# Causal masks of the attention scores: matmuls on TensorE replaced by GpSimd's selects for units 0 to 2, and two products with the values one part later

## Chip, core and metric

The kernel runs on one core of a Trainium2 chip. The metric is the device time of one execution in microseconds (us). Five engines work at once, each with its own queue in program order: TensorE (PE, its weight loads PEld), VectorE (DVE), ScalarE (ACT), GpSimd (POOL) and SyncE (SP, which issues the DMAs). They wait for each other through semaphores.

## The reference

A layer over x of shape (16, 1024, 256), fp32: a state-space block, a gated feed-forward block, attention, and the feed-forward block again, each on the layer-normed x and added to it. The change lies in the attention:

```python
x_proj = x @ Wqkv + bqkv
q = x_proj[:, :, :C].reshape(B, n_head, T, hd)          # C 256, n_head 16, hd 16, T 1024
k = x_proj[:, :, C:2 * C].reshape(B, n_head, T, hd)
v = x_proj[:, :, 2 * C:].reshape(B, n_head, T, hd)
att = jnp.einsum('bhtd,bhsd->bhts', q, k) * (1.0 / jnp.sqrt(jnp.float32(hd)))
causal = jnp.tril(jnp.ones((T, T), dtype=bool))
att = jnp.where(causal, att, jnp.float32(-jnp.inf))
att = jax.nn.softmax(att, axis=-1)
y = att @ v
y = jnp.transpose(y, (0, 2, 1, 3)).reshape(B, T, C)
return y @ Wproj + bproj
```

Since the reshape has no transpose before it, a "head" is a stretch of 64 tokens with 16 pieces of each token as its rows, 1024 rows of 16 numbers in all.

## The kernel before

`attention_phase` works in 64 **slots**, four (q = 0 to 3) for each of 16 **batches** b; a slot handles four heads, in two row groups g of TensorE with two heads p each. Two passes over the causal scores run at once. Pass 1 (`first_piece`, L1981) makes the scores of a later slot with queries on the partitions, and VectorE takes their row maxima (`maxima`, L1737 and L1740); the maxima are turned and moved by DMA into a row of the query stack. Pass 2 (`second_piece`, L2001) makes this slot's scores with keys on the partitions, less the row maximum; ScalarE takes the exponentials (`exponentiate`, L1862) into the tiles `probs`, of which there are three sets (PROBS = 3), used by units in turn. TensorE multiplies these with the values (`times_v`, L2029) into one PSUM bank, `o_ps`.

Pass 2 of a slot has nine **units** (PASS2): stretches of a key block against queries, 512 columns together. Each is done four times (p and g), so a slot has 36 score pieces and 36 exponentials, in 18 steps of two. Units 0, 1, 2, 7 and 8 touch the diagonal, where keys lie above the query within a block of 128. There, before the change, two more small bf16 matmuls per piece (`masked`, L1951) add -1e30 in PSUM above the diagonal: 40 in a slot. Units 0 and 7 have one such block, units 1, 2 and 8 two (128 moving columns in place of 64). Exponentials then become 0.

TensorE's order is written out by hand in its `slot`: behind every third pair of score pieces a **part** ends (12 parts, 0 to 11). There stands at most one **step** of other work through the single bank `x_ps` (`x_events`: transposes of the heads, of y, the output product, the eight projection steps j = 0 to 7 of a later half batch), and then, where TIMES_V_SLOTS says so, a unit's product with the values. Before, units 0 to 7 stand at the parts 2, 3, 4, 5, 7, 8, 10, 11, unit 8 at part 0 of the next slot. The second piece of unit 2 is multiplied with unit 3. ScalarE or VectorE empties `x_ps` after each step and frees it for the next. A unit's exponentials may overwrite `probs` only when the product of three units before is done; for unit 5 that is unit 3's product, since it reads the rest of unit 2.

Projection steps 0 and 1 transpose the normed x, ScalarE copies that to `full`, and GpSimd rounds it to a high part (L1550) and subtracts (L1552, `split`); step 2 (`project`, L2056) waits on TensorE for both splits. GpSimd's queue is another hand-written order, sorted by a place counted in steps: splits, the values' bias (L1616), the residual's bias (`bias`, L1621, behind a DMA), layer norm of x (L1535) and the lay-outs (L1564) that turn the staged q and k for a slot further on, each after its own DMA. ScalarE, VectorE and SyncE are sorted in the same way.

## Time and profile before

| | us |
|---|---|
| median of 3 runs | 3762.44 (3750.83 to 3772.56) |
| the profiled execution | 3763.16 |
| its span, first to last instruction | 3761.3 |
| TensorE busy, of the span | 3560.0 (95%) |
| VectorE busy | 2952.9 (79%) |
| ScalarE busy | 2183.7 (58%) |
| GpSimd busy | 1666.4 (44%) |

The attention stage lies between some 1060 and 3140 us of the span. A batch of four slots takes about 128 us in its steady middle. "Busy" of TensorE is modelled from starts, and overlapping matmuls count once; so the distance from one instruction's start to another's is the better measure of what TensorE does. Idle time of an engine stands before the instruction that ended it, with what released it.

### The profile page before, as it was taken

What the parts mean: (1) busy time and instruction counts of PE and PEld (TensorE: products, weight loads), DVE (VectorE), ACT (ScalarE), POOL (GpSimd) and SP (SyncE); (2) the same over time, 40 slices, a digit from 0 to 9 for tenths busy, and PEclk for the clock granted to TensorE, in tenths of its full rate; (3) what the DMA queues carried; (4) which work ended last, traced back from release to release, by engine and by line L of the source; (5) the groups of instructions that cost most, each with busy time, mean ns of one, the idle gap of its engine ahead of it and who ended that gap; (6) DMA issues with size and microseconds to landing.
All of it is one profiled execution on the core that took longest, in us unless ns stands there. A gap on an engine that the chain in (4) does not pass through costs nothing. (4 is left out here: it accounts for less than half of the span.)

```text
span 3761.3 us, 76026 instructions
## 1 busy us (share of the span) xinstructions
PE 3560.0 (95%) x25550; PEld 2347.9 (62%) x25550; DVE 2952.9 (79%) x9275; ACT 2183.7 (58%) x4151; POOL 1666.4 (44%) x2027
## 2 busy tenths in 40 slices
PE   6999899999689999999999999999999998999997
PEld 5888666666455665566656656655666555666664
DVE  8998666766688888888888888888888893676775
ACT  1110456655337766766676667667667665656654
POOL 2332123223345556656555565565565511223323
PEclk9999899999879999999999999999999999999999
DMA  2333112111497978787887879788887832121211
GB/s 74 100 98 109 57 46 68 54 59 35 116 140 111 126 115 129 120 127 123 122 127 119 132 116 126 116 119 123 124 134 121 120 41 80 40 68 46 68 46 45
DMA packets 694291, 361.16 MB, mean 96 GB/s; under 512 B 297905, under 2 KB 660913, under 8 KB 693937
## 3 DMA queue, kind: packets, MB, share of 16 engines
q1 hardware_dynamic: 693936, 356.62, 53.5%
q8 instruction: 200, 3.28, 0.4%
q14 instruction: 155, 1.26, 0.2%
HBM read 204.49 MB, written 150.99 MB: 95 GB/s over the span
## 5 line engine op out<-in xcount | busy, mean ns | idle before, releaser
L1862 ACT ACTIVATE att_probs<-att_s 128x512 f32<-128x512 f32 x2304 | 1212.5, 601 | 461.2 <-PE att_s L2001 234.4
L1737 DVE CUSTOM_DVE_ANT_0 att_s<-att_s,att_above 128x384 f32<-128x384 f32 (+3 forms) x2048 | 950.2, 519 | 132.8 <-PE att_s L1981 127.1
L1981 PE MATMUL att_s<-att_ks,att_qs 48*128 48x512 f32 (+3 forms) x3072 | 896.0, 401 | 5.7 <-DVE att_maxima L1740 3.6
L2001 PE MATMUL att_s<-att_qs,att_ks 49*128 49x512 f32 (+3 forms) x3072 | 852.4, 373 | 20.5 <-DVE att_maxima L1737 5.2
L2001 PEld LDWEIGHTS att_s<-att_qs,att_ks 49*128 49x128 f32 x3072 | 487.6, 186 | 464.0 <-ACT att_probs L1862 271.6
L1740 DVE TENSOR_REDUCE att_maxima<-att_s 128x1 f32<-128x512 f32 x1024 | 661.9, 684 | 98.3 <-PE att_s L1981 93.2
L2029 PE MATMUL att_o_ps<-att_probs,att_vs 128*32 128x512 f32 (+3 forms) x6144 | 620.5, 497 | 25.1 <-ACT att_probs L1862 22.1
L1981 PEld LDWEIGHTS att_s<-att_ks,att_qs 48*128 48x128 f32 x3072 | 485.9, 189 | 26.4 <-DVE att_maxima L1737 8.9
L1097 PE MATMUL ffn_h2p<-ffn_h,ffn_w 128*128 128x512 f32 x768 | 365.0, 598 | 3.0 <-ACT ffn_h L968 0.9
L1951 PE MATMUL att_s<-att_mask,att_places 64*128 64x128 bf16 (+1 forms) x2560 | 327.7, 212 | 0.0
L1737 DVE DVE_READ_ACCUMULATOR2_ANT att_maxima<- 128x1 f32 x2048 | 293.0, 143 | 0.0
L946 ACT ACTIVATE ffn_uv<-ffn_uvp 128x512 f32<-128x512 f32 x256 | 153.1, 598 | 237.5 <-PE ffn_uvp L1072 237.5
L2029 PEld LDWEIGHTS att_o_ps<-att_probs,att_vs 128*32 128x32 f32 x6144 | 145.9, 108 | 222.9 <-issue 159.6
L1564 POOL CAST att_qs<-att_staged 113x1024 fp32r<-113x1024 f32 x128 | 253.7, 2005 | 0.0
L976 ACT ACTIVATE ffn_h<-ffn_turned,ffn_b 128x512 f32<-128x512 f32 x384 | 241.9, 684 | 13.5 <-PE ffn_turned L1088 11.6
L1564 POOL CAST att_ks<-att_staged 113x1024 fp32r<-113x1024 f32 x126 | 249.7, 2000 | 0.0
L968 ACT ACTIVATE ffn_h<-ffn_h2p,ffn_b 128x512 f32<-128x512 f32 x192 | 132.0, 687 | 197.8 <-PE ffn_h2p L1097 197.8
L1088 PEld LDWEIGHTS ffn_turned<-identf,ffn_uv 128*128 128x128 f32 x1536 | 174.8, 142 | 75.5 <-issue 53.9
L158 ACT ACTIVATE ssm_xnT<-ssm_turned 128x512 fp32r<-128x512 f32 x64 | 34.9, 595 | 313.7 <-PE ssm_turned L166 313.7
L1088 PE MATMUL ffn_turned<-identf,ffn_uv 128*128 128x128 f32 x1536 | 201.8, 274 | 10.2 <-DVE ffn_uv L823 8.0
L823 DVE SCALAR_TENSOR_TENSOR ffn_uv<-ffn_uv,ffn_c_pos 128x256 f32<-128x256 f32 x512 | 209.3, 483 | 2.3
L691 POOL TENSOR_TENSOR ffn_var_eps<-ffn_moments,ffn_eps 128x4 f32<-128x4 f32 x64 | 13.3, 208 | 433.4 <-DVE ffn_moments L776 433.4
(292 smaller groups left out, 6384.8 us busy)
## 6 DMA issues: line engine op xcount, KB each, us to landing
att_staged<-qk_scratch SPq DMA_DIRECT2D x768, 128.0 KB, 7.6
qk_scratch<-att_parts SPq DMA_DIRECT2D x128, 512.0 KB, 3.4
ffn_x<-x SPq DMA_DIRECT2D x64, 512.0 KB, 5.2
ssm_x<-in_L_attn_a_x_dram SPq DMA_DIRECT2D x32, 512.0 KB, 3.7
x<-ssm_y SPq DMA_DIRECT2D x32, 512.0 KB, 3.0
x<-ffn_y SPq DMA_DIRECT2D x32, 512.0 KB, 2.9
att_x<-x SPq DMA_DIRECT2D x32, 512.0 KB, 7.4
v_scratch<-att_v_tok SPq DMA_DIRECT2D x32, 512.0 KB, 5.3
```

Source lines behind the costliest of these rows:

```text
L823: last = v.scalar_tensor_tensor(out=new[:, t, 0:D], in0=old[:, t, D:2 * D], scalar=c_pos[i][j][:, t, k:k + 1], in1=old[:, t, 0:D], op0=ALU ...
L976: last = a(h1[k][:, f, :], turned_ps[:, f, :], ACT.Gelu, bias=b1[:, f:f + 1])
L1088: last = pe.transpose(turned_ps[:, f, t * P:(t + 1) * P], of[:, t, f * P:(f + 1) * P], identf[:, :])
L1097: last = mm(h2_ps[:, :], w2[:, f, :], h1[k][:, f, :], start=(f == 0), stop=(f == KT - 1))
L1564: last = g.tensor_copy(stack[0:ROWS, :].rearrange("p (t c) -> p t c", c=HD)[:, e * n:(e + 1) * n, :], staged[side][0:ROWS, :, e * n:(e + 1 ...
L1737: last = v.tensor_tensor_reduce(scores, scores, above[:, CH - w:CH], 1.0, -3.0e38, ALU.add, ALU.max, to)
L1740: last = v.tensor_reduce(to, scores, AX.X, ALU.max)
L1862: a(probs[u % PROBS][2 * g + p][:, 0:n], bank[:, 0:n], ACT.Exp).then_inc(exp_done, 1)
L1951: last = mm(blocks[:, at, GROUP * half:GROUP * (half + 1)], places[rows, 2 * (1 - k) + half, :], mask[rows, 1 - k, 0:len(cols), :], start= ...
L1981: last = mm(bank[:, col:col + w], rows_of(qs[buf], g, KROWS, p, BT * blk, BT * (blk + 1)), rows_of(ks[buf], g, KROWS, p, t0, t1), start=k ...
L2001: last = mm(bank[:, col:col + w], rows_of(ks[buf], g, SHIFT + 1, p, BT * j, BT * (j + 1)), rows_of(qs[buf], g, SHIFT + 1, p, t0, t1), star ...
L2029: last = mm(o_ps[32 * i:32 * i + 32, HD * (t0 - first_t):HD * (t1 - first_t)], vs[s][:, NBLK * head + j, :], probs[of % PROBS][i][:, col:c ...
```

## The change

For units 0, 1 and 2 of every slot (SELECTED) the two mask matmuls of a piece are gone, and `stop` moves to the last score matmul. In their place GpSimd sets the entries above the diagonal of the exponentials in `probs` to zero, one `affine_select` in place for each of the 12 pieces (`keep_causal`), behind a wait for the exponential, at a place 1.4 steps behind it in GpSimd's order. `times_v` of these units waits for the selects and no longer for the exponentials. Units 7 and 8 keep their mask matmuls.

The products of units 3 and 5 move from parts 5 and 8 to parts 6 and 9. The steps through `x_ps` that stood at parts 6 and 9 move to parts 5 and 8 (one from 8 to 7), and with them their copies, splits, additions and stores on the other queues. The residual's bias in the second slot of a batch moves from place 4 to 7.1 on GpSimd, and the first two lay-outs from 6.3 and 7.6 to 7.2 and 8.2.

```diff
+    SELECTED = ((0, 1, 2),) * 4
-    PROBS = 3
+    PROBS, KEPT_BEHIND = 3, 1.4
-    TIMES_V_SLOTS = {2: 0, 3: 1, 4: 2, 5: 3, 7: 4, 8: 5, 10: 6, 11: 7}
+    TIMES_V_SLOTS = {2: 0, 3: 1, 4: 2, 6: 3, 7: 4, 9: 5, 10: 6, 11: 7}
-    LAY_OUT_AT, LAY_OUT_BEHIND_X_AT, PIECES = (6.3, 7.6, 10.2, 12.2), (8.2, 8.4, 11.2, 11.4), 2
+    LAY_OUT_AT, LAY_OUT_BEHIND_X_AT, PIECES = (7.2, 8.2, 10.2, 12.2), (8.2, 8.4, 11.2, 11.4), 2
-        finish = [] if first else {0: [(3, "turn", 0), (6, "out", 0), (7, "turn", 1), (9, "out", 1), (10, "turn", 2)],
-                                   1: [(1, "out", 2), (2, "turn", 3), (6, "out", 3)]}.get(q, [])
-        project = {0: [(1, 6), (4, 7)], 1: [(4, 0), (7, 1), (9, 2)], 2: [(1, 3), (4, 4), (6, 5), (9, 6)],
+        finish = [] if first else {0: [(3, "turn", 0), (5, "out", 0), (7, "turn", 1), (8, "out", 1), (10, "turn", 2)],
+                                   1: [(1, "out", 2), (2, "turn", 3), (5, "out", 3)]}.get(q, [])
+        project = {0: [(1, 6), (4, 7)], 1: [(4, 0), (7, 1), (8, 2)], 2: [(1, 3), (4, 4), (5, 5), (8, 6)],
                    3: [(1, 7)]}[q] if more else []
-        project += [(2, 0), (4, 1), (6, 2), (8, 3), (9, 4), (11, 5)] if q == 3 and more2 else []
+        project += [(2, 0), (4, 1), (5, 2), (7, 3), (8, 4), (11, 5)] if q == 3 and more2 else []
...
+                def keep_causal(quad, step, g):
+
+                    u, p = step // 2, step % 2
+                    pool.wait_ge(exp_done, 2 * STEPS * quad + 2 * step + g + 1)
+                    cols = diagonals(PASS2[u], False)
+                    m = blocks_at(probs[u % PROBS][2 * g + p][:, :], cols)
+                    nc.gpsimd.affine_select(out=m, in_=m, pattern=[[0, len(cols)], [1, P]], compare_op=ALU.is_ge, fill=0.0,
+                                            base=0, channel_multiplier=-1).then_inc(causal_kept, 1)
...
-                        tasks += [((17.5, 4)[q], lambda: bias(b - 1, 2 + q))]
+                        tasks += [((17.5, 7.1)[q], lambda: bias(b - 1, 2 + q))]
...
+                    for of, units, ahead in ((quad - 1, SELECTED[(q - 1) % 4], STEPS), (quad, SELECTED[q], 0)):
+                        for step, group in itertools.product((2 * u + p for u in units for p in range(2)), range(2)):
+                            at = step + group / 2 + KEPT_BEHIND - ahead
+                            if of >= 0 and (at >= 0 if ahead else at < STEPS):
+                                tasks += [(at, lambda of=of, step=step, group=group: keep_causal(of, step, group))]
...
-                              stop=k == len(PASS2[u]) - 1 and not diagonals(PASS2[u], False))
+                              stop=k == len(PASS2[u]) - 1 and (u in SELECTED[buf] or not diagonals(PASS2[u], False)))
                     if k == len(PASS2[u]) - 1:
-                        if diagonals(PASS2[u], False):
+                        if diagonals(PASS2[u], False) and u not in SELECTED[buf]:
                             last = masked(bank[:, :], 1, g, diagonals(PASS2[u], False))
...
-                    pe.wait_ge(exp_done, 2 * STEPS * quad + 4 * u + 4)
+                    if u in SELECTED[q]:
+                        pe.wait_ge(causal_kept, kept_before(quad, u) + 4)
+                    else:
+                        pe.wait_ge(exp_done, 2 * STEPS * quad + 4 * u + 4)
```

## Rows read from the trace of the kernel before

**Rows 1.** The page: busy time of the engines, and two costly groups.
```profile
PE 3560.0 (95%) x25550; PEld 2347.9 (62%) x25550; DVE 2952.9 (79%) x9275; ACT 2183.7 (58%) x4151; POOL 1666.4 (44%) x2027
...
L1862 ACT ACTIVATE att_probs<-att_s 128x512 f32<-128x512 f32 x2304 | 1212.5, 601 | 461.2 <-PE att_s L2001 234.4
...
L1564 POOL CAST att_qs<-att_staged 113x1024 fp32r<-113x1024 f32 x128 | 253.7, 2005 | 0.0
```

**Rows 2.** Sums over one steady batch; columns: stretch, length, engines' busy us, clock, DMA.
```profile
1860.23:1988.60 128.37, 125.57 (x1116) 77.65 (x1112) 111.58 (x374) 89.88 (x171) 76.87 (x68) 1.00 0.83 124
```

**Rows 3.** Timeline of TensorE, second slot, parts 3 to 6: start, length, engine, what, count.
```profile
1901.67 0.38 PE L2001 MATMUL att_s<-att_qs,att_ks 49*128 49x256 f32 x1
...
1902.88 0.66 PE L2070 MATMUL att_x_ps<-identf,att_o 128*128 128x128 f32 x4
...
1904.47 0.50 PE L2001 MATMUL att_s<-att_qs,att_ks 49*128 49x512 f32 x1
...
1905.43 0.55 PE L2052 MATMUL att_x_ps<-identf,att_x 128*128 128x128 f32 x3
...
1907.23 0.50 PE L2001 MATMUL att_s<-att_qs,att_ks 49*128 49x512 f32 x1
...
1908.60 1.50 PE L2029 MATMUL att_o_ps<-att_probs,att_vs 128*32 128x512 f32 x16 [0.40 <-ACT att_probs L1862]
...
1910.03 0.50 PE L2001 MATMUL att_s<-att_qs,att_ks 49*128 49x512 f32 x1
```

**Rows 4.** The same timeline, parts 8 and 9.
```profile
1916.35 1.07 PE L2029 MATMUL att_o_ps<-att_probs,att_vs 128*32 128x512 f32 x8
...
1917.35 0.50 PE L2001 MATMUL att_s<-att_qs,att_ks 49*128 49x512 f32 x1
...
1918.77 0.50 PE L2056 MATMUL att_x_ps<-att_xnT,att_wqkv 128*128 128x512 f32 x1
```

**Rows 5.** The mask products, grouped by line: duration ns min/median/max.
```profile
L1951 PE MATMUL att_s<-att_mask,att_places x2560: 190/216/327, 1082.8 to 3134.2; 64*128 64x128 bf16 x119, 64*128 64x64 bf16 x78
```

**Rows 6.** Sums as in rows 2, over parts 0 to 3 of the first and third slot.
```profile
1860.23:1871.34 11.11, 11.11 (x126) 7.80 (x122) 10.18 (x31) 7.84 (x15) 3.03 (x3) 1.00 0.90 125
...
1924.87:1935.37 10.50, 10.50 (x118) 6.96 (x114) 9.69 (x33) 7.34 (x14) 2.91 (x4) 1.00 1.22 140
```

**Rows 7.** Selects and copies of GpSimd by group, then GpSimd's and VectorE's timeline.
```profile
L53 POOL TENSOR_SCALAR_AFFINE_SELECT identf<-identf 128x128 f32<-128x128 f32 x1 | 0.3, 296 | 0.2 <-POOL identb L50 0.2
...
L1535 POOL TENSOR_SCALAR att_x<-att_x,att_moments,att_rstd 128x256 f32<-128x256 f32 x116 | 140.9, 1222 | 3.1
...
1036.62 2.40 DVE L1712 CAST att_ks<-att_staged 113x2048 fp32r<-113x2048 f32 x1
...
1036.92 2.27 POOL L1601 TENSOR_SCALAR_AFFINE_SELECT att_mask<-att_mask 64x128 bf16<-64x128 bf16 x1
```

**Rows 8.** Timelines of TensorE and GpSimd, fourth slot, parts 4 and 5.
```profile
1968.23 0.66 PE L2052 MATMUL att_x_ps<-identf,att_x 128*128 128x128 f32 x4
...
1969.38 0.49 PE L2001 MATMUL att_s<-att_qs,att_ks 49*128 49x512 f32 x1
...
1971.00 1.28 PE L2029 MATMUL att_o_ps<-att_probs,att_vs 128*32 128x512 f32 x12 [0.32 <-ACT att_probs L1862]
...
1965.16 1.28 POOL L1552 TENSOR_TENSOR att_xnT<-att_full,att_xnT 128x512 fp32r<-128x512 f32 x1
...
1970.63 1.27 POOL L1552 TENSOR_TENSOR att_xnT<-att_full,att_xnT 128x512 fp32r<-128x512 f32 x1
```

**Rows 9.** Timelines of TensorE and GpSimd, second slot: transposes of step 1 and its split.
```profile
1913.87 0.66 PE L2052 MATMUL att_x_ps<-identf,att_x 128*128 128x128 f32 x4
...
1916.26 1.28 POOL L1552 TENSOR_TENSOR att_xnT<-att_full,att_xnT 128x512 fp32r<-128x512 f32 x1
```

**Rows 10.** Timelines of GpSimd and TensorE, third slot, part 3.
```profile
1931.90 1.28 POOL L1552 TENSOR_TENSOR att_parts<-att_full,att_parts 128x512 fp32r<-128x512 f32 x1
...
1934.36 1.07 PE L2029 MATMUL att_o_ps<-att_probs,att_vs 128*32 128x384 f32 x16
```

More of the change, by code:

```diff
@@ L4 @@
 from contextlib import ExitStack
+import itertools
 import numpy as np
@@ L1331, in attention_phase @@
          xn_ready, x_full, x_free, hi_ready, parts_ready, v_ready, v_stored, s1_full, s1_free, row_max_ready,
-         row_max_turned, s2_full, exp_done, pv_done, o_free, recip_ready, bias_added, tail_full, y_done, yT_done, out_added) = [sem("att_" + n) for n in (
+         row_max_turned, s2_full, exp_done, pv_done, o_free, recip_ready, bias_added, tail_full, y_done, yT_done, out_added, causal_kept) = [sem("att_" + n) for n in (
              "low_free v_free wq_loaded loaded const_ready zero_max weights_ready mask_zero mask_ready above_ready rounded split_done stats_done moments_done eps_added rstd_ready "
              "xn_ready x_full x_free hi_ready parts_ready v_ready v_stored s1_full s1_free row_max_ready "
-             "row_max_turned s2_full exp_done pv_done o_free recip_ready bias_added tail_full y_done yT_done out_added").split()]
+             "row_max_turned s2_full exp_done pv_done o_free recip_ready bias_added tail_full y_done yT_done out_added causal_kept").split()]
         wq_raw = y_sb[:, :, :, :].rearrange("p f n d -> p (f n d)")[:, 0:KT * 3 * D].rearrange("p (k n) -> p k n", k=KT)
@@ L1372, in s2_use, with kept_before, diagonals, blocks_at @@
             return 2 * STEPS * q + 2 * step + g
+        def kept_before(quad, u):
+            of = [4 * len(units) for units in SELECTED]
+            units = SELECTED[quad % 4]
+            return sum(of) * (quad // 4) + sum(of[:quad % 4]) + (4 * units.index(u) if u in units else 0)
+        def diagonals(unit, end):
+            cols, col = [], 0
+            for blk, t0, t1 in unit:
+                w = HD * (t1 - t0)
+                if (t1 == BT * (blk + 1)) if end else (t0 == BT * blk):
+                    cols.append(col + w - P if end else col)
+                col += w
+            return cols
+        def blocks_at(bank, cols):
+            at = slice(cols[0] // P, cols[-1] // P + 1, max(1, (cols[-1] - cols[0]) // P))
+            return bank.rearrange("p (n w) -> p n w", w=P)[:, at, :]
         def in_order(tasks):
@@ L1668, in _ @@
                 run(pool, sequence)
+                for step, group in itertools.product((2 * u + p for u in SELECTED[3] for p in range(2)), range(2)):
+                    if step + group / 2 + KEPT_BEHIND >= STEPS:
+                        keep_causal(4 * NB - 1, step, group)
                 for r in range(4):
@@ L1953, in masked @@
                     return last
-                def diagonals(unit, end):
-                    cols, col = [], 0
-                    for blk, t0, t1 in unit:
-                        w = HD * (t1 - t0)
-                        if (t1 == BT * (blk + 1)) if end else (t0 == BT * blk):
-                            cols.append(col + w - P if end else col)
-                        col += w
-                    return cols
                 def first_wait(quad, unit, g):
```

## The prediction

> **What bounds the kernel now.** I read the page first [rows 1], then the sums of one steady batch [rows 2], then TensorE's own timeline, part by part [rows 3]. The page says TensorE 95%. The batch sums say it for the stage that the change touches: of 128.37 us TensorE is busy 125.57, VectorE 111.58 (87%), ScalarE 89.88, GpSimd 76.87 (60%), clock 1.00 throughout. So the time of a batch is TensorE's list of work plus its waits, and VectorE stands right behind it. Sixteen such batches (64 slots) are the attention stage. Nothing before or behind it changes.
>
> In the timeline I take the distance from the first score product of a part to the first instruction behind the scores. Part 3 of the second slot goes from 1901.67 to 1902.88: 1.21 us with six mask products. Part 4 has none: 1904.47 to 1905.43, 0.96. Part 5 has none either and takes 1907.23 to 1908.60, 1.37: 0.41 us of wait for exponentials, in front of unit 3's product with the values, which then runs 1.43 us, until 1910.03 [rows 3]. Part 9 has four masks of 64 columns and takes 1.42 us, from 1917.35 to 1918.77 [rows 4], where 0.96 and some 0.1 for the masks would do: 0.36 of wait. The part before it held only scores and one product with the values (1916.35 to 1917.35 [rows 4]), 1.9 us in all, while VectorE's share of a batch is 111.58 / 48 = 2.3 us a part. There are five waits of this kind in a batch, at parts 8 and 9, of 0.35 to 0.48. These two kinds of wait are what the moves of the products and steps touch.
>
> **The change, part by part** (us for the four slots of a batch; minus is a gain).
>
> *Masks removed.* 24 of 40 mask products per slot, all in parts 0 to 3. A mask is listed with 0.19 us or more [rows 5], but they overlap, so I price the part: 1.21 - 0.96 = 0.25 for six masks of 128 columns [rows 3]. Parts 0 and 1 hold narrower ones; I price them by columns at 0.16 and 0.22. Sum 0.88 a slot, 3.5 a batch, if TensorE sets the pace there. VectorE speaks against all of it: in parts 0 to 3 it is busy 9.69 of 10.50 us in the third slot and 10.18 of 11.11 in the first (the second is the same kind, the fourth looser) [rows 6]. Less 0.88 the third slot would have 9.62 us for 9.69 of work. So I take back 0.4 in the third slot, 0.3 in the second, 0.1 in each other one: **-2.6**, bounds -3.5 (all) and -1.5 (VectorE needs its usual gaps too).
>
> The Trainium skill ("TensorE: Matmul & The Clock Gate", Back-to-back issue gap) gives N/2.4 + 2.5 ns for one product behind another, 29 and 56 ns at 64 and 128 columns: by it 8 and 16 masks would be worth 1.1 us a slot. The rows say 0.25 for six, some 42 ns each, less than its 56; by the page the term would be -4.5 before VectorE's part.
>
> *Unit 3's product one part later.* Its 0.41 of wait goes in three slots; in the fourth it is larger: scores from 1969.38, product at 1971.00, 1.62 against 0.96 [rows 8]. **-1.9**. Cover: the exponentials it needs are then a whole part old.
>
> *A new wait behind it.* The exponential of unit 5's first piece must not overwrite the probabilities that unit 3's product still reads (second piece of unit 2, same buffer). That exponential is the last of part 6, and the product is now at the end of part 6: it starts 0.96 + 1.43 + 0.1 = 2.5 us into the part instead of after 1.6. It takes 0.6 [rows 1], done at 3.1; the third score piece of part 7 wants its bank two thirds into that part's scores, at about 2.4 + 0.6 = 3.0. Bounds 0 and 0.4 a slot, I take 0.2 (the bank waits for the semaphore too): **+0.8**.
>
> *Short parts.* Part 8 now holds an output, a projection step or the like, part 9 is short instead. The five waits at parts 8 and 9 come to 2.0; behind the new part 9 (1.07 + 1.0, a little longer than 1.9) and the third slot's short parts 6 and 7 I expect 1.0 in all to be left: **-1.0**, bounds 0 and -1.6.
>
> *Steps one part earlier.* In the second slot the projection step 2 moves from part 9 to 8, in the fourth from 6 to 5. Each needs GpSimd's split of step 1, which sits in the part just before. Fourth slot: step 1's transposes start at 1968.23, ScalarE's copy and GpSimd's cast and subtraction end at 1970.63 + 1.27 = 1971.90, 3.67 us later; TensorE's scores of part 5 would be over at 1969.38 + 0.96 = 1970.34 [rows 8]. It waits 1.6. Second slot: from the transposes at 1913.87 to the end of the subtraction at 1916.26 + 1.28 is 3.67 too [rows 9], 1917.54; the scores of part 8 were over at 1916.35 [rows 4], so 1.2, and 0.7 more, my estimate, since GpSimd's bias and four lay-outs of 2.0 us [rows 1] now begin behind the selects. **+3.5**, bounds +2.8 and +4.3. The other moved steps only need the shared PSUM bank, freed well within a part: 0; uncovered, a copy's 0.6 us each.
>
> *Selects on GpSimd.* 12 a slot. A select of 128x128 fp32 took 296 ns; for the eight with two blocks I take 0.49, an estimate between once and twice that, bounds 0.3 and 1.22 (another operation on 128x256) [rows 7]. That is 5.2 us a slot, 76.87 + 20.8 = 98 of 128: it fits. Who waits is TensorE's unit product. Unit 0 to 2's products come a part behind their last exponential, 2 us or more. Only where GpSimd is held is it close: third slot, split until 1931.90 + 1.28 = 1933.18, then three selects to 1934.65, product at 1934.36 less the masks' gain [rows 10]: 0.3 and more, part of it in place of a wait that the next part has now; I take 0.3. Fourth slot: split until 1965.16 + 1.28 = 1966.44, four selects to 1968.4, product half a microsecond before the scores of 1969.38, less the gain [rows 8]: 0.1. **+0.4**, bounds 0 and +6.
>
> *Bias and lay-outs behind the selects.* The lay-outs are needed a slot later, the bias only by the output in part 5; before, GpSimd sat idle for that load. 0. Semaphores and their queue: nothing else stands behind the waiting product but the next scores, priced above.
>
> **Sum.** -2.6 - 1.9 + 0.8 - 1.0 + 3.5 + 0.4 = -0.8 a batch. Fifteen batches: -12. The last has no projection: its slots save 4 us. The profiled execution took 3763.16 us (span 3761.3), within 1 us of the median 3762.44; minus 16 that is 3747, and 3746 against the median.
>
> **Rivals.**
> *A. TensorE keeps the whole gain.* VectorE has slack in the other parts and three banks to run ahead, so the masks bring 3.5, the short parts 1.0, unit 3 1.9, and the exponential's new wait is hidden; the splits still cost 3.5: -2.9 a batch, 15 x 2.9 + 4 = 48, **3714**. For it: VectorE at 87%. Against: VectorE's 9.69 of 10.50.
> *B. VectorE becomes the bound and the splits add (slower).* Place: parts 0 to 3, where VectorE is 91 to 92% busy, and the splits at parts 5 and 8. Masks -1.5, unit 3 -1.9, short parts 0, exponential +0.8, splits +4.3, selects +0.8: +2.5 a batch, **3797**. It decides once splits and selects cost more than the 4.5 that masks, unit 3 and short parts bring; the step 1 to step 2 gap in the fourth slot shows it.
> *C. GpSimd is late.* If the two-block select takes 1.22 us, four behind the split in the fourth slot end at 1971.3, 2.5 behind the product, as in the third slot, and 1 in the second: +6 a batch, **3835**. It starts at 0.6 a select. For it: one 64x128 select took 2.27 us, beside siblings of 0.3. But it began at 1036.92 inside VectorE's copy from SBUF to SBUF (1036.62, 2.40 long) and ended with it [rows 7], and in the steady batches VectorE reads mostly PSUM.
> The Trainium skill ("SBUF — State Buffer", Who interferes with whom) has it as a rule: VectorE in a two-port mode shuts GpSimd out for a whole instruction, with at most one SBUF input and no such mode it does not. By it C would need such copies; the trace's 2.27 agrees.
> *D. Nothing to see,* as waits only move: 3762.
>
> **How the numbers follow.** Forecast (about 3730 to 3760) 0.42; A 0.27; B 0.21; C 0.06; D 0.04. Faster than 3743.6 (0.5%, about what a measurement here can tell) is A and a third of the forecast's case: 0.42. Within 0.5%: the rest of the forecast, D, and a little of B: 0.36. Slower: 0.22. The range goes from just under A to just under B's price, 3706 to 3792; the likeliest case's own range is 3728 to 3762.
>
> **What would show it.** Right: parts 0 to 3 without masks near 1.0 us; no wait before unit 3's product; TensorE idle 1 to 2 us before the projection step 2, ended by GpSimd's subtraction; selects of 0.3 and 0.5 us; VectorE over 88% of the batch. Wrong: step 2 starting without a wait, selects over 0.6 us, products of units 0 to 2 waiting for selects in every slot, or the slots shorter by a whole microsecond each.

## The result, and the profile after

The changed kernel takes 3775.99 us (median of 20 runs, 3764.94 to 3787.72), the kernel before 3764.92 beside it (20 runs): ratio 1.0028, with 95% between 1.0019 and 1.0037. So it is 0.3% slower, a difference that is certain in its sign and smaller than the 0.5% of the prediction's bound. The forecast was 3746 us, a small gain. The profiled execution took 3777.97 us with a span of 3775.6; the one before, 3763.16 with 3761.3.

The page of the kernel after, busy times with the clock line, and the group of the selects:

```profile
PE 3549.2 (94%) x24014; PEld 2289.0 (61%) x24014; DVE 2958.7 (78%) x9275; ACT 2182.9 (58%) x4151; POOL 1926.7 (51%) x2795
...
PEclk9999899999779999999989999999999988999999
...
L1641 POOL TENSOR_SCALAR_AFFINE_SELECT att_probs<-att_probs 128x256 f32<-128x256 f32 (+1 forms) x768 | 272.6, 369 | 358.2 <-ACT att_probs L1903 345.2
```

TensorE has 1536 instructions fewer than in [rows 1], 24 in each of 64 slots, yet is busy only 10.8 us less, and the span is 14 us longer. VectorE and ScalarE do what they did. GpSimd is busy 260 us more, the selects' 272.6 less some 12 that its other work took less. Whether TensorE waits for them is asked in e2 and e8.

The sums over slots, in the form of [rows 2]: the first, third and fourth slot of the batch shown there, and the second of a later batch, which is nearer to the median:

```profile
1860.56:1892.02 31.46, 31.41 (x272) 19.36 (x268) 28.67 (x96) 22.43 (x43) 21.36 (x27) 1.00 1.04 128
2158.82:2192.53 33.71, 31.66 (x254) 18.47 (x250) 27.95 (x93) 21.84 (x43) 21.51 (x27) 0.95 0.68 110
1931.89:1962.81 30.92, 30.52 (x250) 17.59 (x247) 27.47 (x96) 22.26 (x42) 23.80 (x30) 0.97 0.79 127
1962.81:1997.89 35.08, 33.64 (x266) 19.92 (x262) 27.26 (x92) 23.86 (x45) 26.69 (x34) 0.95 0.52 103
```

The second and the fourth slot are long, and the granted clock there is 0.95, where [rows 2] had 1.00 over the whole batch. (The third has 0.97 here, because the second slot of its batch, one of 39.9 us, ended at half clock.) From the starts of the slots on TensorE's timeline I take the median length of each over batches 1 to 14 and the mean of the whole batch, for the kernels of this study (us; "half" counts stretches in which the granted clock was 0.50):

| kernel | slot 1 | 2 | 3 | 4 | sum of medians | mean batch | half |
|---|---|---|---|---|---|---|---|
| before | 32.75 | 31.47 | 30.89 | 33.47 | 128.58 | 129.38 | 3 |
| after | 31.46 | 33.75 | 30.01 | 35.07 | 130.29 | 129.93 | 19 |
| e1, step 2 back | 31.46 | 33.05 | 30.01 | 35.23 | 129.75 | 129.43 | 21 |
| e2, masks only | 31.98 | 30.77 | 30.82 | 32.74 | 126.31 | 126.09 | 0 |
| e3, moves only | 32.24 | 32.15 | 30.08 | 34.30 | 128.77 | 129.33 | 5 |
| e4, wait filled | 31.46 | 32.34 | 30.01 | 33.55 | 127.36 | 127.14 | 1 |
| e5, mixed | 31.47 | 30.76 | 30.00 | 32.74 | 124.97 | 124.77 | 0 |
| e6, split later | 31.98 | 30.76 | 30.82 | 32.74 | 126.30 | 126.14 | 1 |
| e7, tail masks | 31.99 | 30.75 | 30.82 | 32.74 | 126.30 | 126.09 | 0 |
| e8, selects twice | 32.09 | 31.66 | 34.09 | 36.86 | 134.70 | 134.43 | 26 |
| e9, measured later | 31.39 | 30.77 | 30.41 | 32.75 | 125.32 | 125.07 | 1 |
| e10, both later | 31.41 | 30.77 | 30.04 | 32.74 | 124.96 | 124.65 | 0 |

The means add up to the span: 14 x (129.93 - 129.38) = 7.7 us, and the last batch, 119.4 against 113.3, gives 6.1; 13.8 of the 14.3 us between the two spans. The medians tell what the usual slot does. The two differ because the execution of before has a few long batches (131.9 and 133.9 against 128.6), and because not every slot of after is long. That the clock is lower is no accident of the one profiled execution: over the whole span it is 0.962 to 0.969 in all 20 executions of the changed kernel, and 0.974 to 0.980 in the 23 executions of the kernel before that stood beside e1 to e4.

Slots 1 and 3 gained 1.3 and 0.9; slots 2 and 4, where the projection step 2 moved forward, lost 2.3 and 1.6. The timelines of TensorE and GpSimd over parts 5 and 6 of a fourth slot show how (the places of [rows 8]):

```profile
1974.16 0.66 PE L2086 MATMUL att_x_ps<-identf,att_x 128*128 128x128 f32 x4
...
1975.41 0.49 PE L2032 MATMUL att_s<-att_qs,att_ks 49*128 49x512 f32 x1
...
1977.98 2.90 PE L2090 MATMUL att_x_ps<-att_xnT,att_wqkv 128*128 128x512 f32 x6 [1.36 <-POOL att_xnT L1576]
1980.81 0.73 PE L2032 MATMUL att_s<-att_qs,att_ks 49*128 49x512 f32 x1
...
1973.30 1.49 POOL L1641 TENSOR_SCALAR_AFFINE_SELECT att_probs<-att_probs 128x256 f32<-128x256 f32 x4
1975.87 0.61 POOL L1574 CAST att_xnT<-att_full 128x512 fp32r<-128x512 f32 x1 [1.09 <-ACT att_full L1913]
1976.57 1.26 POOL L1576 TENSOR_TENSOR att_xnT<-att_full,att_xnT 128x512 fp32r<-128x512 f32 x1
```

From the transposes of step 1 (1974.16) to the end of GpSimd's subtraction (1976.57 + 1.26 = 1977.83) it is 3.67 us, the prediction's number, and TensorE starts step 2 right behind it, after 1.36 us of idle time. That is the forecast wait. What was not forecast is the length of step 2 itself: 2.83 us until the next scores at 1980.81. Sums over the two stretches:

```profile
1975.40:1977.90 2.50, 1.22 (x12) 0.85 (x8) 2.49 (x10) 2.37 (x5) 1.94 (x3) 1.00 0.33 106
1977.98:1980.81 2.83, 2.83 (x7) 1.80 (x8) 0.22 (x2) 0.00 (x0) 2.83 (x2) 0.50 0.00 0
```

During the wait the granted clock is still 1.00. Behind it, while TensorE is busy without a gap, it is 0.50, which is 1.2 GHz in place of 2.4. The waits in this trace between 1110 and 2900 us (total, times, longest):

```profile
PE att_x_ps L2090 <- POOL att_xnT L1576: 48.2, 28, 2.8
```

28 waits, 1.7 us on average, two a batch: 1.36 us in every fourth slot, 1.97 to 2.76 in every second one. Before, no such wait is in the list. In batches 1 to 14 there are 27 of them, and behind 18 the clock falls: 10 of 13 in fourth slots, 8 of 14 in second ones. A fourth slot in which it stays up is 33.6 us long in place of 35.1, and step 2 in it takes 1.56 us.

### The profile page after: what moved, and what is told of

Read it like the earlier page. It is cut to its first block and busy times, and to the rows that moved or that the text cites. A ratio compares the mean times of both kernels' runs of the same rounds, so it can differ in the third digit from the quotient of the medians.

```text
span 3775.6 us, 73723 instructions
## 1 busy us (share of the span) xinstructions
PE 3549.2 (94%) x24014; PEld 2289.0 (61%) x24014; DVE 2958.7 (78%) x9275; ACT 2182.9 (58%) x4151; POOL 1926.7 (51%) x2795
## 5 line engine op out<-in xcount | busy, mean ns | idle before, releaser
L2012 PE MATMUL att_s<-att_ks,att_qs 48*128 48x512 f32 (+3 forms) x3072 | 880.4, 397 | 6.7 <-DVE att_maxima L1781 4.3
L2032 PEld LDWEIGHTS att_s<-att_qs,att_ks 49*128 49x128 f32 x3072 | 471.6, 190 | 508.9 <-ACT att_probs L1903 317.9
L2063 PE MATMUL att_o_ps<-att_probs,att_vs 128*32 128x512 f32 (+3 forms) x6144 | 628.5, 504 | 6.7 <-POOL att_probs L1641 6.0
L2012 PEld LDWEIGHTS att_s<-att_ks,att_qs 48*128 48x128 f32 x3072 | 475.9, 192 | 26.1 <-DVE att_maxima L1778 9.0
L1641 POOL TENSOR_SCALAR_AFFINE_SELECT att_probs<-att_probs 128x256 f32<-128x256 f32 (+1 forms) x768 | 272.6, 369 | 358.2 <-ACT att_probs L1903 345.2
L2090 PE MATMUL att_x_ps<-att_xnT,att_wqkv 128*128 128x512 f32 x714 | 216.2, 442 | 50.1 <-POOL att_xnT L1576 50.1
L970 ACT ACTIVATE ffn_h<-ffn_h2p,ffn_b 128x512 f32<-128x512 f32 x192 | 131.9, 687 | 198.5 <-PE ffn_h2p L1099 198.5
```

The costliest lines, as they stand in the source:

```text
L1641: nc.gpsimd.affine_select(out=m, in_=m, pattern=[[0, len(cols)], [1, P]], compare_op=ALU.is_ge, fill=0.0, base=0, channel_multiplier=-1).t ...
L2012: last = mm(bank[:, col:col + w], rows_of(qs[buf], g, KROWS, p, BT * blk, BT * (blk + 1)), rows_of(ks[buf], g, KROWS, p, t0, t1), start=k ...
L2032: last = mm(bank[:, col:col + w], rows_of(ks[buf], g, SHIFT + 1, p, BT * j, BT * (j + 1)), rows_of(qs[buf], g, SHIFT + 1, p, t0, t1), star ...
L2063: last = mm(o_ps[32 * i:32 * i + 32, HD * (t0 - first_t):HD * (t1 - first_t)], vs[s][:, NBLK * head + j, :], probs[of % PROBS][i][:, col:c ...
L2090: last = mm(bank[:, :], wq[i][:, f, cols], xnT[k][:, f, :], start=(n == 0), stop=(n == KT * len(PARTS_R) - 1))
```

## The experiments

The theory: the moves brought step 2 so close to its split that TensorE stands still, and the stop costs twice, as a wait and as half a clock behind it. Rivals: the selects delay the products (C of the prediction); the new exponential wait or the busy VectorE is what costs (B). The runs of e1 to e4 stood beside a median of 3754.97 us for the kernel before, e5 to e8 beside 3762.07, e9 and e10 beside 3764.04, so compare by ratio across these groups.

**e1: the changed kernel with step 2 back at its old parts.**

```diff
-        project = {... 1: [(4, 0), (7, 1), (8, 2)], ...
-        project += [(2, 0), (4, 1), (5, 2), (7, 3), (8, 4), (11, 5)] if q == 3 and more2 else []
+        project = {... 1: [(4, 0), (7, 1), (9, 2)], ...
+        project += [(2, 0), (4, 1), (6, 2), (7, 3), (8, 4), (11, 5)] if q == 3 and more2 else []
```

> The changed kernel, with only projection step 2 put back one part later (part 9 in the second slot, part 6 in the fourth). Theory S (the loss is TensorE's wait for GpSimd's split of step 1, and the half clock that follows it): both waits go, TensorE's clock stays at 1.00 in the steady batches, second slot about 31 us and fourth about 33; a batch goes from 130.3 to some 125 us, the kernel to about 3710 us, 1.5% below before. Rival G (GpSimd's selects hold up products or VectorE): the waits in front of step 2 go, but the slots stay near 33 and 34 us, and the kernel stays at 3765 to 3776 us.

Measured: 3751.32 us, ratio 0.9986 (0.9973 to 0.9999), where some 3710 was expected of the theory. The wait for the split is gone but for three second slots, the half clock is not (21 stretches), and slots 2 and 4 stay long at 33.05 and 35.23. The profiled execution is the slowest of its 12 (3769.68 us), but the clock over the span is 0.961 to 0.971 in all of them. The timeline of TensorE and two sums in e1's fourth slot, part 5, which now holds scores only, and part 6:

```profile
1963.31 0.50 PE L2032 MATMUL att_s<-att_qs,att_ks 49*128 49x512 f32 x1 [0.23 <-ACT att_probs L1903]
...
1964.07 0.46 PE L2032 MATMUL att_s<-att_qs,att_ks 49*128 49x512 f32 x1 [0.26 <-DVE att_maxima L1778]
...
1964.83 0.76 PE L2032 MATMUL att_s<-att_qs,att_ks 49*128 49x512 f32 x1 [0.26 <-ACT att_probs L1903]
...
1965.67 2.93 PE L2090 MATMUL att_x_ps<-att_xnT,att_wqkv 128*128 128x512 f32 x6
1968.52 2.79 PE L2063 MATMUL att_o_ps<-att_probs,att_vs 128*32 128x512 f32 x16
```
```profile
1964.00:1967.50 3.50, 3.16 (x9) 2.23 (x10) 2.65 (x10) 1.22 (x3) 3.50 (x4) 0.58 0.00 0
1967.50:1972.00 4.50, 4.50 (x24) 1.41 (x22) 0.10 (x1) 0.56 (x2) 0.74 (x1) 0.56 0.00 0
```

So my edit took one wait away and made others: with neither a product nor a step in part 5, TensorE runs into the exponentials and the row maxima, three waits of a quarter of a microsecond within 1.6 us, and the clock is at half around and behind these too. Step 2 takes 2.85 us again and unit 3's product, 1.43 in [rows 3], takes 2.7. It does not isolate the wait for the split, then; what it shows is that the clock also falls where TensorE waits for something else.

**e2: the masks alone** (selects, their waits and the places of bias and lay-outs, with the old order of products and steps). **e3: the moves alone** (the kernel before with the new order).

```diff
# e2, from the changed kernel; e3 puts the lines marked - into the kernel before
-    TIMES_V_SLOTS = {2: 0, 3: 1, 4: 2, 6: 3, 7: 4, 9: 5, 10: 6, 11: 7}
+    TIMES_V_SLOTS = {2: 0, 3: 1, 4: 2, 5: 3, 7: 4, 8: 5, 10: 6, 11: 7}
-        finish, project = ...    # the lists of x_events, new
+        finish, project = ...    # the lists of x_events, as before
```

> Only the selects in place of the masks (with the places of GpSimd's bias and lay-outs that belong to them); products with the values and all steps through x_ps stand as before the change. Theory S: the selects are free and the masks' time comes off, 0.5 to 0.7 us a slot; about 3725 to 3735 us. Rival G: products wait for selects and GpSimd's splits come late; 3760 us or more. If VectorE is the bound of parts 0 to 3, less than 0.3 us a slot: 3750 us.

> The kernel before with only the products of units 3 and 5 one part later and the steps through x_ps one part earlier; masks on TensorE as before, no selects. Theory S: the second and fourth slot wait 1.2 to 1.7 us in front of projection step 2, the clock halves for a few us behind it, slots one and three gain 0.4 to 0.6; about 3810 us, slower than the changed kernel. Rival G: without selects the moves gain what was meant, 3740 us or less, and there is no half clock.

Measured: e2 3714.00 us, ratio 0.9885 (0.9869 to 0.9900); e3 3767.21, ratio 1.0030 (1.0020 to 1.0041). The two halves have opposite signs. The masks alone bring 1.15%: per slot 0.77, 0.70, 0.07 and 0.73 us, 2.27 a batch. (1.15% is 43 us, 2.9 a batch: before also has stops and three stretches at half clock in its steady batches, and e2 has none of the latter, so the mean batches differ by 3.3.) The moves alone bring 0.5 in slot 1 and 0.8 in slot 3 and lose 0.7 and 0.8 in slots 2 and 4; their loss is far from the 3810 that was expected. Their waits, over the same stretch:

```profile
PE att_x_ps L2056 <- POOL att_xnT L1552: 36.5, 28, 2.0
```

28 waits again, but the clock falls behind only 4 of the 27 in batches 1 to 14. In second slots the wait is mostly 1.1 us, not 2.0, and none of these 14 waits is followed by half clock. What is shorter there is GpSimd's side: from the transposes of step 1 to the end of the subtraction it is 3.5 us, against 4.4 in the changed kernel, while TensorE's scores of part 8 begin 1.58 us behind those transposes in both. GpSimd's timeline, a second slot of the changed kernel, then one of e3, which keeps bias and lay-outs at their old places:

```profile
2177.03 3.95 POOL L1588 CAST att_ks<-att_staged 113x1024 fp32r<-113x1024 f32 x2
2180.94 0.60 POOL L1574 CAST att_xnT<-att_full 128x512 fp32r<-128x512 f32 x1
```
```profile
1781.63 1.99 POOL L1564 CAST att_ks<-att_staged 113x1024 fp32r<-113x1024 f32 x1
1784.39 0.61 POOL L1550 CAST att_xnT<-att_full 128x512 fp32r<-128x512 f32 x1 [0.77 <-ACT att_full L1872]
```

ScalarE's copy of step 1 ends at 2179.98 in the first and at 1784.33 in the second. With the lay-outs behind the selects, the split of step 1 stands behind one of them for 0.96 us; in e3 it starts at once. These 0.9 us are the prediction's 0.7 for the second slot.

In fourth slots the wait is the same 1.36 us, and 4 of 13 are followed by half clock, against 10 with the masks gone. This is a count in one execution each, but the clocks of all executions agree: over the span 0.971 to 0.976 in the 12 of e3, 0.962 to 0.969 in the 20 of the changed kernel. So the length of the wait is not all that decides. The two halves of the change work against each other: 126.31 + 128.77 - 128.58 would be 126.5 a batch, and together they take 130.3. Slot by slot the same sum gives 31.5, 31.5, 30.0 and 33.6; the changed kernel has 31.5, 33.8, 30.0 and 35.1, so all of the difference lies in the two slots with the waits.

**e4: the changed kernel, with twelve transposes of the identity in front of step 2's wait.** They go into `x_ps`, and step 2 overwrites them.

```diff
+                            for n in range(12):
+                                pe.transpose(bank[:, (n % 4) * P:(n % 4 + 1) * P], identf[:, :], identf[:, :])
                             (before the wait for the split in step 2)
```

> The changed kernel with 12 transposes of the identity into the idle x_ps bank (some 1.7 us of work) in front of the wait for the split before each projection step 2 in the slots; nothing else moves, what they write is overwritten. Theory S with the clock as a part of its own: the wait stays as long (the engine is now busy in it), the half-clock stretches of 3.4 us behind it mostly vanish, step 2 takes 1.6 us and not 2.8; about 25 us less than the changed kernel, 3750. Rival (the clock is no cause, only the wait counts): the same time as the changed kernel or, by what the transposes outlast the split, up to 20 us more.

Measured: 3733.13 us, ratio 0.9938 (0.9921 to 0.9954), 0.9% or some 34 us under the changed kernel by the ratios, although TensorE has 348 instructions more. The clock over the span is 0.973 to 0.978 in its six executions. TensorE's timeline, parts 5 and 6 of a fourth slot:

```profile
1953.26 0.50 PE L2032 MATMUL att_s<-att_qs,att_ks 49*128 49x512 f32 x1
...
1954.38 1.53 PE L2084 MATMUL att_x_ps<-identf 128*128 128x128 f32 x12
1955.73 1.65 PE L2092 MATMUL att_x_ps<-att_xnT,att_wqkv 128*128 128x512 f32 x6
1957.32 0.50 PE L2032 MATMUL att_s<-att_qs,att_ks 49*128 49x512 f32 x1
```

and in front of step 2 in a second slot:

```profile
1900.07 1.53 PE L2084 MATMUL att_x_ps<-identf 128*128 128x128 f32 x12
1902.09 1.67 PE L2092 MATMUL att_x_ps<-att_xnT,att_wqkv 128*128 128x512 f32 x6 [0.49 <-POOL att_xnT L1576]
```

The transposes take 1.35 us, about what the wait took, so step 2 starts no sooner. But it takes 1.59 us in place of 2.83, and there is one stretch at half clock in batches 1 to 14. In the second slot half a microsecond of idle time remains, and the clock stays up too. This separates the two costs: after minus e4, 130.29 - 127.36 = 2.9 us a batch (1.4 in slot 2, 1.5 in slot 4, nothing in the others), is the clock; e4 minus e2, 1.05 a batch, is the moves with their waits. And e4's slots are the sums of the two halves, 31.5, 31.5, 30.0 and 33.6, but for 0.9 more in the second, which is the split behind the lay-out.

**e5: the mixed order.** Selects in all slots, the new order in slots 1 and 3, the old one in 2 and 4.

```diff
-    TIMES_V_SLOTS = {2: 0, 3: 1, 4: 2, 6: 3, 7: 4, 9: 5, 10: 6, 11: 7}
+    TIMES_V_SLOTS = ({2: 0, 3: 1, 4: 2, 6: 3, 7: 4, 9: 5, 10: 6, 11: 7}, {2: 0, 3: 1, 4: 2, 5: 3, 7: 4, 8: 5, 10: 6, 11: 7}) * 2
-                                   1: [(1, "out", 2), (2, "turn", 3), (5, "out", 3)]}.get(q, [])
+                                   1: [(1, "out", 2), (2, "turn", 3), (6, "out", 3)]}.get(q, [])
-        project = {... 1: [(4, 0), (7, 1), (8, 2)], ...
+        project = {... 1: [(4, 0), (7, 1), (9, 2)], ...
-        project += [(2, 0), (4, 1), (5, 2), (7, 3), (8, 4), (11, 5)] if q == 3 and more2 else []
+        project += [(2, 0), (4, 1), (6, 2), (8, 3), (9, 4), (11, 5)] if q == 3 and more2 else []
```

> The changed kernel's order in the first and third slot of a batch only; the second and fourth slot keep the products of units 3 and 5, the output and projection step 2 where they were before the change (masks are selects in all four). Theory W (a slot loses where a part has to wait for the split or is left without other work, and the moves are good where this is not so): slots 31.5, 30.8, 30.0 and 32.7 us, clock 1.00 in the steady batches, a batch 125.0, some 1.3 less than with the masks' change alone; about 3694 us. Rival (the moves' gain in slots one and three is paid back in the slot behind them): 3714 us, as the masks' change alone.

Measured: 3701.58 us (3698.93 to 3702.14), ratio 0.9833 (0.9813 to 0.9853). It beats both kernels, by 60 us the one before; by the ratios some 20 us of that are the order (against e2), the rest are the masks. Sums over the four slots and the batch:

```profile
1833.23:1864.71 31.48, 31.43 (x272) 19.38 (x268) 28.68 (x96) 22.43 (x43) 21.40 (x27) 1.00 1.02 129
1864.71:1895.45 30.74, 30.25 (x254) 17.68 (x250) 27.68 (x93) 21.85 (x43) 21.55 (x27) 1.00 0.64 103
1895.45:1925.84 30.39, 30.00 (x252) 17.09 (x248) 27.98 (x100) 22.26 (x42) 23.83 (x30) 1.00 1.12 163
1925.84:1958.58 32.74, 32.25 (x264) 19.12 (x261) 27.11 (x92) 23.77 (x45) 26.75 (x34) 1.00 0.64 116
1833.23:1958.58 125.35, 123.93 (x1028) 73.26 (x1025) 111.45 (x374) 90.31 (x172) 93.52 (x117) 1.00 0.85 128
```

Each slot has the better of its two lengths and the clock is 1.00 throughout. In the third slot VectorE is busy 27.98 of 30.39 us, the highest share (92%) of the four.

**e6: why the masks bring nothing in the third slot.** e2, with the split of the projection step 3 in the third slot 1.6 steps later on GpSimd, so that it comes behind unit 1's selects. **e9 and e10:** e5 with VectorE's measurements of the next x (`MEASURE_AT`) later, and e9 with the later split too.

```diff
# e6 and e10
-     tasks += [(at + 2, lambda j=which, n=n: split(projected(b, q, j)[0], j, x_base(b, q) + n))]
+     tasks += [(at + (3.6 if (q, which) == (2, 3) else 2), lambda j=which, n=n: split(...))]
# e9 and e10
-    MEASURE_AT, MOMENTS_AT = (2.6, 4.1, 5.6, 7.1), 8.6
+    MEASURE_AT, MOMENTS_AT = (6.1, 7.6, 9.1, 10.6), 11.6
```

> The masks' change alone, with GpSimd's split of projection step 3 in the third slot behind the selects of unit 1 and not before them. If the third slot got only 0.1 us from the masks because unit 1's product waits there for selects that stand behind this split, part 3 of that slot goes from 1.44 to 0.9 us and the slot from 30.8 to 30.3; 15 x 0.5 = 8 us, about 3706 us. Rival (VectorE is the bound of these parts, as the prediction had it): the wait moves to part 4 and the slot stays at 30.8; 3714 us.

> The mixed order (selects in all slots, the moves in the first and third slot only) with VectorE's four statistics instructions of the next x, 0.41 us each, in the first and third slot 3.5 steps later in its queue (places 6.1 to 10.6, moments at 11.6, in place of 2.6 to 7.1 and 8.6). If VectorE is what keeps the third slot from gaining by the masks (its waits of 0.5 in part 3 and 0.2 in part 4), these fall and the slot goes from 30.0 to about 29.5 us, the first slot, without such a wait, stays at 31.5; about 3693 us against 3701 for the mixed order. Rival (selects behind the split are the cause): the slot stays at 30.0, or the wait comes back in parts 7 to 9; 3701 us or more.

> As the run before, and GpSimd's split of projection step 3 in the third slot behind the selects of unit 1. If both VectorE's lag and the selects behind the split hold the third slot, and each alone hides the other, only this one shows the gain: part 3 at 0.95 and part 4 at 1.0 us, the slot at 29.3; about 3690 us. If one of them is the cause alone, it is the same as the run before or as the mixed order.

Measured: e6 3715.72 us, ratio 0.9877 (0.9851 to 0.9902), as e2. TensorE's timeline, third slot, parts 3 and 4, of e2 and then of e6:

```profile
2161.09 0.38 PE L2032 MATMUL att_s<-att_qs,att_ks 49*128 49x256 f32 x1
...
2162.53 1.07 PE L2063 MATMUL att_o_ps<-att_probs,att_vs 128*32 128x384 f32 x16 [0.44 <-POOL att_probs L1641]
2163.53 0.50 PE L2032 MATMUL att_s<-att_qs,att_ks 49*128 49x512 f32 x1
...
2164.72 1.21 PE L2090 MATMUL att_x_ps<-att_xnT,att_wqkv 128*128 128x512 f32 x4
```
```profile
2159.07 0.38 PE L2032 MATMUL att_s<-att_qs,att_ks 49*128 49x256 f32 x1
...
2160.00 1.07 PE L2063 MATMUL att_o_ps<-att_probs,att_vs 128*32 128x384 f32 x16
2161.13 0.47 PE L2032 MATMUL att_s<-att_qs,att_ks 49*128 49x512 f32 x1
...
2162.70 1.66 PE L2090 MATMUL att_x_ps<-att_xnT,att_wqkv 128*128 128x512 f32 x6
```

In e2 unit 1's product waits 0.44 us for the selects; from the scores of part 3 to step 4 it is 3.63 us. In e6 that wait is gone, part 3's scores take 0.93 in place of 1.44, but part 4's take 1.57 in place of 1.19, and from scores to step 4 it is 3.63 again. GpSimd's lateness, forecast at 0.3 us here, is real and costs nothing, since the time comes back as waits in the next part. e9, 3712.92 (0.9866, 0.9842 to 0.9889), has third slots of 30.41, longer than e5's: part 3 waits as in e2, and the relief in part 4 (0.95) comes back in parts 6 and 8 (1.27 and 1.36). e10, 3702.33 (0.9845, 0.9822 to 0.9869), has both edits and 30.04, e5's length to 0.04. So e6 and e10 move the waits and leave the slot as long as it was, and e9 makes it longer. With the moves the slot takes 30.0 us and VectorE is busy 28.0 of it in the median (93%). That VectorE sets the pace there is what these runs speak for; none took work off VectorE, so it is not shown. And it is not the whole answer for the masks alone: in e2 VectorE has the same 27.9 us of work in a slot of 30.8.

**e7: the last batch keeps its masks on TensorE** (e2 otherwise). The last batch of e2 has half clock in 37.5 us of its 124.3, of before in none of 113.3, and the theory was that the lost masks had thinned TensorE's work too far there.

```diff
+        def selected(quad):
+            return SELECTED[quad % 4] if quad < 4 * (NB - 1) else ()
```

> The masks' change alone, but the last batch keeps its masks on TensorE, as before the change. That batch has little other work for TensorE: with selects it took 124.3 us, at half clock for 48 of them, against 113.3 before. If the masks' absence leaves TensorE idle there and the clock follows, the last batch comes back to about 113 us with under 5 us at half clock; about 3704 us. Rival (the half clock there comes from something else, the state of the engine's earlier work): last batch still 120 us or more, 3714 us.

Measured: 3722.25 us, ratio 0.9883 (0.9858 to 0.9908), no better than e2; its last batch took 121.3 us, 20.5 of them at half clock. And e6, which has e2's order in the last batch, took 112.5 us there with 3.4 at half clock. The theory falls: the last batch's clock differs between executions of the same order, each of them profiled once. What decides it stays open; it is a matter of some 12 us that no reading of the steady batches contains.

**e8: each select done twice** (e2 otherwise), the second behind a semaphore of the first.

```diff
-                    nc.gpsimd.affine_select(...).then_inc(causal_kept, 1)
+                    for done in (causal_half, causal_kept):
+                        nc.gpsimd.affine_select(...).then_inc(done, 1)
+                        if done is causal_half:
+                            pool.wait_ge(causal_half, kept_before(quad, u) + 2 * p + g + 1)
```

> The masks' change alone, with each select done twice, the second behind the first's semaphore: about 0.55 us more for each of 12 a slot, 6.6 us a slot, GpSimd at some 95% of a batch. It asks how much cover the selects have. If GpSimd's work is covered up to its time in total, products of units 1 and 2 wait some tenths in the third and fourth slot: 3720 to 3735 us. If what counts is the order in GpSimd's queue (rival C of the prediction), products and splits wait 1 to 2 us in several slots and the clock halves behind them: 3790 us or more.

Measured: 3850.65 us, ratio 1.0225 (1.0200 to 1.0250), by the ratios some 128 us over e2. TensorE's waits for selects, 1110 to 2900 us, in e2 and in e8:

```profile
PE att_o_ps L2063 <- POOL att_probs L1641: 5.7, 13, 0.4
```
```profile
PE att_o_ps L2066 <- POOL att_probs L1642: 58.3, 33, 2.7
```

Single selects leave 5.7 us of waiting between 1110 and 2900 us; a second one makes it 58.3, and there are 26 stretches at half clock, 24 of them close behind such a wait. It falls where the prediction looked for it: slots 3 and 4, by 3.3 and 4.1 us. So rival C is a live mechanism with its point between once and twice the measured select, and the change stays on the good side of it.

## Why the prediction was wrong, point by point

The total missed by 30 us, and the direction with it. Per batch, forecast against measured (differences of the sums of medians, and in brackets of the mean batches, in which before carries its own long ones):

| term | forecast | measured | from |
|---|---|---|---|
| masks with the selects' waits | -2.6 + 0.4 = -2.2 | -2.3 (-3.3) | e2 - before |
| moves: unit 3, short parts, exponential, split waits | -1.9 - 1.0 + 0.8 + 3.5 = +1.4 | +1.05 (+1.05) | e4 - e2 |
| clock behind the split waits | not in the sum | +2.9 (+2.8) | after - e4 |
| sum | -0.8 | +1.7 (+0.55) | after - before |

**Masks: right, with the shares wrong.** In the first slot the scores went from 1.21 to 0.99 us in part 2 and to 0.90 in part 3. By my shares the slots had 0.78, 0.58, 0.48 and 0.78 to give; they gave 0.77, 0.70, 0.07 and 0.73. The place for which VectorE spoke (9.69 us of work in 10.50, [rows 6]) is the one where the gain is lost, and all of it is; that VectorE is the reason is not shown (e6, e9, e10). The bounds held.

**Selects: right.** A select of two blocks takes 0.41 us in the median (0.49 assumed), of one block 0.29, the shortest 0.28 (0.30, [rows 7]):

```profile
L1641 POOL TENSOR_SCALAR_AFFINE_SELECT att_probs<-att_probs x768: 282/406/425, 1081.4 to 3132.7; 128x256 f32<-128x256 f32 x128, 128x128 f32<-128x128 f32 x64
```

None of 768 is longer than 0.425: what held one for 2.27 us in [rows 7] does not happen in the steady batches, as argued. The Trainium skill's rule on who shuts out whom ("SBUF — State Buffer", Who interferes with whom) stands with both readings. Products waited for selects 5.7 us in e2 (above), 0.4 a batch, the forecast's number; it cost nothing in the third slot, where it stood. The term of 0 for bias and lay-outs behind the selects holds only beside the 0.7 that the second slot's split was given for them, and that was 0.9 (e3).

**Unit 3 and the short parts: right.** By the prediction's terms a slot without a split has -0.41 for unit 3, some -0.25 for its short parts and +0.2 for the exponential, -0.5 in all. Slot 1 brought 0.5. Slot 3 brought 0.8, since two of its parts, 8 and 9, lose their wait (1.39 and 1.42 us of scores in e2, 1.07 and 1.05 in e5), where slot 1 has one (e5 - e2).

**The exponential of unit 5: right place, a little more.** In the first slot of the kernel after, ScalarE's timeline, then TensorE's, parts 6 and 7:

```profile
1879.45 2.07 ACT L1903 ACTIVATE att_probs<-att_s 128x512 f32<-128x512 f32 x4 [0.96 <-PE att_o_ps L2063]
...
1879.26 0.49 PE L2032 MATMUL att_s<-att_qs,att_ks 49*128 49x512 f32 x1
...
1880.54 0.66 PE L2111 MATMUL att_x_ps<-identf,att_y 128*128 128x128 f32 x4
```

The exponential starts when unit 3's product ends; part 7 takes 1.28 us from scores to step, against 0.96 before: 0.32 a slot for the 0.2 that was taken, within its bounds.

**Steps one part earlier: the step that failed.** The prediction has it that TensorE waits 1.6 us in the fourth slot and 1.9 in the second, +3.5 in all with bounds 2.8 and 4.3, and leaves it at that. The waits came as said, 1.36 and 2.0 us. But the term prices a wait as the time it lasts and puts what the clock does behind it at nothing, without a reason. There step 2 takes up to 2.83 us for 1.59, and what follows until the clock is back is slow as well: 2.9 us a batch (after - e4), more than the 0.8 that the whole change was to bring.

The trace of before had the row that would have told. I read one steady batch with its clock of 1.00 [rows 2] and took that for the whole stage, as the clock line of the page seems to say. But that line has tenths of slices of 94 us. An earlier batch of the same trace has a stop inside a projection step, TensorE's timeline and the sums around it, of before:

```profile
1422.44 0.74 PE L2056 MATMUL att_x_ps<-att_xnT,att_wqkv 128*128 128x512 f32 x2
1424.65 1.98 PE L2056 MATMUL att_x_ps<-att_xnT,att_wqkv 128*128 128x512 f32 x4 [1.47 <-issue]
1426.56 0.79 PE L2001 MATMUL att_s<-att_qs,att_ks 49*128 49x512 f32 x1
```
```profile
1423.10:1424.60 1.50, 0.08 (x1) 0.00 (x0) 1.03 (x5) 0.50 (x2) 0.89 (x1) 1.00 1.56 147
1424.60:1428.20 3.60, 3.55 (x11) 2.10 (x11) 0.70 (x3) 1.50 (x3) 0.71 (x2) 0.53 0.99 71
```

One wait of 1.47 us, and behind it the clock at 0.53 and four products in 1.91 us; the slot around it took 33.8 us, 2.9 over its median, twice what the wait lasted. It is one of five stops over 0.5 us in batches 1 to 14 of before: the clock fell at this one and at one of 2.78 us, and not at those of 0.55, 0.81 and 1.29. With twice the wait as the price of the two splits of a batch, the term would have been 3.5 x 2 = 7.0 and the forecast +2.7 a batch, 3800: too much, since the clock falls at two waits in three, but of the right sign. The measured +1.7 (+0.55) lies between.

The Trainium skill ("TensorE: Matmul & The Clock Gate", HAM oscillation) warns of gaps in the middle of a kernel that send TensorE's clock back to half; the prediction used another rule of that page, on gaps between products, and not this one. The runs agree on the effect, but the gaps that had it here, 1.36 us and in e1 a few of 0.25, are shorter than those the section warns of.

Without the clock the moves would have cost 1.05 and the change would have brought 1.2 a batch, near the forecast's 0.8 (e4 is 0.6% or 23 us below before, the forecast 16).

**The rivals.** A (3714) was wrong for the changed kernel. e2 shows the same number, but beside a faster group of runs: by its ratio it stands for 3719 on the prediction's scale, and no step is moved there. B (3797) had the sign and the place (the splits at parts 5 and 8) but not the mechanism: the gain of the masks was lost in the third slot alone, the short parts gained, and nothing of B is the clock. C: not this change, see e8. D: the times nearly agree with it, the slots do not: two are shorter by a microsecond, two longer by two.

## What to carry to other kernels

On a TensorE that sets the pace, price a new wait as the wait plus the slower clock behind it: search the trace for stops that are already there and read the granted clock of the stretch behind one, not of the one that idles. Where work moves earlier, compare the distance to its producer slot by slot: the same reordering was worth 0.5 to 0.8 us in two slots of this kernel and cost 2 to 3 in the other two, and keeping each slot's better order gave some 20 us over the masks alone. Two edits can cost together what neither costs alone (here 3.8 us a batch over their sum), so time them apart and together.

## What the runs showed of the hardware

- The granted clock fell from 1.00 to 0.50 at single waits of 1.36 us in 10 fourth slots of 13 (after), and at waits of the same length in 4 of 13 with the mask products still on TensorE (e3). What decides in a single case stays open.
- Three waits of 0.23 to 0.26 us close together, in a part of scores alone, had half clock around and behind them too, 0.58 and 0.56 (e1).
- Throw-away transposes in the wait left one stretch at half clock in place of 19 and made the kernel 0.9% faster, some 34 us, with more instructions (e4).
- The last batch of the same order took 124.3 us in one kernel (e2) and 112.5 in another (e6), with 37.5 and 3.4 us at half clock; what decides it is open.
